# Second attention of a four-stage kernel: maxima reduced two banks at a time, scores in a ring of three banks, exponentials over two banks and one

## The reference, cut to what matters

```python
qkv = x @ attn_qkvw + attn_qkvb            # x: 2 x 256 x 512 in the drawn shapes, here 1 x 1024 x 512
qkv = qkv.reshape(B, S, 3, HEADS, hd)      # 32 heads of 16
scores = jnp.einsum('bhqd,bhkd->bhqk', q, k) * scale
probs = jax.nn.softmax(scores, axis=-1)
ctx = jnp.einsum('bhqk,bhkd->bhqd', probs, v)
return ctx @ attn_ow + attn_ob
```

## Time and profile before

| | us |
|---|---|
| median of 3 runs | 1727.81 (1727.61 to 1731.67) |
| the profiled execution, its own time | 1724.92 |
| its span, first to last instruction | 1722.6 |
| PE busy over the span | 1546.5 (90%) |
| DVE busy | 1038.8 (60%) |
| ACT busy | 809.8 (47%) |
| POOL busy | 227.6 (13%) |

### The profile page before, as it was taken

One profiled execution on the slowest core, in us unless ns is written; L12 is line 12 of the kernel. 1 busy time (PEld: TensorE's weight loads), 2 busy tenths in 40 slices (PEclk: granted clock), 3 DMA queues, 4 the chain that ended last, 5 costly groups with the idle time before them and its releaser, 6 DMA issues. The chain is left out here.

```text
span 1722.6 us, 22663 instructions
## 1 busy us (share of the span) xinstructions
PE 1546.5 (90%) x8286; PEld 1012.5 (59%) x8286; DVE 1038.8 (60%) x1801; ACT 809.8 (47%) x1458; POOL 227.6 (13%) x225
## 2 busy tenths in 40 slices
PE   6958999999999999879799989887799888899987
PEld 4736766776666777568688878666343333333355
DVE  5735666666666666445433335642679777889446
ACT  5325666666666666322112122131047555667834
POOL 2751112111111111000000000000000331131100
PEclk9978999999999999989899999989559988989999
DMA  4242212221111211243121210055712245441001
GB/s 129 97 154 70 69 59 66 68 89 65 65 65 59 84 58 32 80 146 107 64 73 56 73 50 1 2 208 184 109 22 41 62 80 84 84 54 23 18 13 43
DMA packets 71714, 125.23 MB, mean 73 GB/s; under 512 B 13054, under 2 KB 38782, under 8 KB 70318
## 3 DMA queue, kind: packets, MB, share of 16 engines
q1 hardware_dynamic: 71540, 123.67, 25.6%
q0 software_dynamic: 64, 0.11, 0.0%
HBM read 87.23 MB, written 33.85 MB: 70 GB/s over the span
## 5 line engine op out<-in xcount | busy, mean ns | idle before, releaser
L1625 DVE TENSOR_REDUCE ah_minus_half<-ah_ring 128x1 f32<-128x512 f32 x512 | 317.2, 679 | 56.6 <-PE ah_ring L1553 56.6
L1608 ACT ACTIVATE ah_probs<-ah_score 128x1024 f32<-128x1024 f32 x256 | 248.8, 1022 | 179.1 <-PE ah_score L1568 178.5
L958 DVE TENSOR_REDUCE mh_minus_max<-mh_score 128x1 f32<-128x128 f32 (+7 forms) x256 | 193.7, 757 | 195.5 <-PE mh_score L772 195.3
L1553 PE MATMUL ah_ring<-ah_k_stack,ah_q_stack 48*128 48x512 f32 x512 | 216.3, 525 | 54.2 <-DVE ah_minus_half L1625 30.2
L1553 PEld LDWEIGHTS ah_ring<-ah_k_stack,ah_q_stack 48*128 48x128 f32 x512 | 98.2, 211 | 237.9 <-DVE ah_minus_half L1625 211.5
L882 ACT ACTIVATE mh_probs<-mh_score,mh_minus_max 128x128 f32<-128x128 f32 (+7 forms) x256 | 189.6, 741 | 35.9 <-DVE mh_minus_max L958 33.4
L1568 PE MATMUL ah_score<-ah_q_stack,ah_k_stack 49*128 49x512 f32 x512 | 167.1, 466 | 6.5 <-DMA ah_q_stack<-ah_rows 4.9
L768 PE MATMUL mh_score<-shared,h_hi 128*128 128x512 f32 (+3 forms) x384 | 151.6, 395 | 2.2 <-ACT mh_probs L882 2.2
L1583 PE MATMUL ah_mix<-ah_probs,ah_v 128*32 128x512 f32 x1024 | 148.5, 654 | 0.6 <-ACT ah_probs L1608 0.6
L1031 POOL TENSOR_TENSOR h_lo<-mh_pe,h_hi 64x512 fp32r<-64x512 f32 x64 | 81.8, 1279 | 469.5 <-ACT h_hi L868 465.9
L769 PE MATMUL mh_score<-shared,h_hi 128*128 128x512 f32 (+3 forms) x384 | 132.1, 344 | 0.0
(11 more groups left out here) (224 smaller groups left out, 2886.7 us busy)
## 6 DMA issues: line engine op xcount, KB each, us to landing
mh_w<-in_w_pairs SPq DMA_DIRECT2D x16, 896.0 KB, 5.5
x<-in_w_inner SPq DMA_DIRECT2D x14, 768.0 KB, 4.1
pe_scratch<-fr_pe_out SPq DMA_DIRECT2D x4, 2048.0 KB, 6.6
mh_pe<-pe_scratch SPq DMA_DIRECT2D x16, 512.0 KB, 3.9
mh_spread<-inverse_scratch SPq DMA_DIRECT2D x64, 128.0 KB, 2.8
a_scratch<-mh_mixed SPq DMA_DIRECT2D x32, 256.0 KB, 2.3
x<-a_scratch SPq DMA_DIRECT2D x8, 1024.0 KB, 5.8
qk_scratch<-shared SPq DMA_DIRECT2D x32, 256.0 KB, 2.0
```

The costliest lines, as they stand in the source:

```text
L958: nc.vector.reduce_max(minus_max[:, s % 4:s % 4 + 1], score_ps[s % 2][:, base:base + width], AX.X, negate=True).then_inc(max_ready, 1)
L1553: return nc.tensor.matmul(ring[:, m % 3, :], q_stack[a][stack_rows(p, PARTS), c, t * P:(t + 1) * P], k_stack[a][stack_rows(p, PARTS), c, h ...
L1608: nc.scalar.activation(probs[:, 2 * (u % 2) + c, :], score_ps[c][:].rearrange("p e n -> p (e n)"), ACT.Exp, scale=MHA_SCALE).then_inc(prob ...
L1625: nc.vector.reduce_max(minus_half[:, m:m + 1], ring[:, m % 3, :], AX.X, negate=True).then_inc(max_taken, 1)
```

## The change

Three things are edited. The eight banks are dealt out anew: `ah_ring` has four banks as two pairs, `ah_score` has three, `ah_mix` keeps one. A maximum is now taken of two heads at once: two matmuls, one semaphore, one DVE reduction over 2 x 512 columns with two results. The score matmuls are numbered 0 to 511 and go to bank `n % 3`; ACT takes the exponential of banks 0 and 1 together and then of bank 2 alone. `probs` has room for three units instead of two. The lead of the maxima is built up by eight per unit instead of seven, all maxima lie at the starts of the two score stages, and DVE inverts sums four maxima later. Last, `Shares.put` no longer waits until POOL has divided the half-group two before, but until the one four before is divided and the one two before is inverted; `c_in` and `spread_in` get a semaphore per group parity for that.

```diff
@@ Shares.put
         sp.wait_ge(out_taken, NHALF * g + half + 1)
-        wait(sp, self.ready, NHALF * (g - 1) + half + 1)
+        wait(sp, self.ready, NHALF * (g - 2) + half + 1)
+        wait(sp, self.inverse_ready, NHALF * (g - 1) + half + 1)
@@ mha_heads
-        probs = sb("probs", [P, 4, 2 * BANK])
-        ring = ctx.enter_context(nc.psum_tensor("ah_ring", [P, 3, BANK], F32))
-        score_ps = [ctx.enter_context(nc.psum_tensor(f"ah_score{i}", [P, 2, BANK], F32)) for i in range(2)]
+        probs = sb("probs", [P, BANKS, BANK])
+        ring = ctx.enter_context(nc.psum_tensor("ah_ring", [P, 2, 2, BANK], F32))
+        score_ps = ctx.enter_context(nc.psum_tensor("ah_score", [P, 3, BANK], F32))
...
+        exps_before = lambda tiles: 2 * (tiles // 3) + (tiles % 3 > 0)
-            at = lambda unit: min(FIRST + 7 * unit, HALF_MAX + LEAD + PER_UNIT * unit, TOTAL)
+            at = lambda unit: min(FIRST + 8 * unit, HALF_MAX + LEAD + PER_UNIT * unit, TOTAL)
             now, then = at(n), at(n + 1)
-            return (now, min(now + (then - now + 1) // 2, then), min(now + (3 * (then - now) + 2) // 4, then))[stage]
+            middle = min(now + 2 * ((then - now + 2) // 4), then)
+            return (now, middle, middle)[stage]
@@ PE
-            def one_maximum(m):
-                wait(pe, max_taken, m - 2)
-                maximum(m).then_inc(max_ready, 1)
+            def two_maxima(m):
+                wait(pe, max_taken, m // 2 - 1)
+                maximum(m)
+                maximum(m + 1).then_inc(max_ready, 1)
...
-                wait(pe, probs_ready, 2 * (NUNIT * g + u) + c - 1)
                 for p in range(2):
+                    n = 4 * (NUNIT * g + u) + 2 * c + p
                     rows = stack_rows(p, PARTS + 1)
-                    last = nc.tensor.matmul(score_ps[c][:, p, :], k_stack[a][rows, c, j * P:(j + 1) * P],
-                                            q_stack[a][rows, c, half * BANK:(half + 1) * BANK], start=True, stop=True)
-                last.then_inc(scores_ready, 1)
+                    if n >= 3:
+                        pe.wait_ge(probs_ready, exps_before(n - 2))
+                    nc.tensor.matmul(score_ps[:, n % 3, :], k_stack[a][rows, c, j * P:(j + 1) * P],
+                                     q_stack[a][rows, c, half * BANK:(half + 1) * BANK], start=True, stop=True
+                                     ).then_inc(scores_ready, 1)
@@ ACT
+            for n in range(4 * UNITS):
+                if n % 3 == 0:
+                    exp(n, 2)
+                    done = n + 2
+                elif n % 3 == 2:
+                    exp(n, 1)
+                    done = n + 1
@@ DVE
-                nc.vector.reduce_max(minus_half[:, m:m + 1], ring[:, m % 3, :], AX.X, negate=True).then_inc(max_taken, 1)
+                nc.vector.reduce_max(minus_half[:, m:m + 2], ring[:, m // 2 % 2, :, :], AX.X, negate=True).then_inc(max_taken, 1)
...
-                if m >= HALF_MAX * (inverted + 1) + LEAD + 13 * PER_UNIT:
+                if m >= HALF_MAX * (inverted + 1) + LEAD + 14 * PER_UNIT:
```

More of the change, by code:

```diff
@@ L1354, in put @@
             first = rows.start + n * HD
-            sp.dma_start(self.c[first:first + HD, cols], out[2 * HD * n:2 * HD * n + HD, g % 2, cols]).then_inc(self.c_in[half], 16)
+            sp.dma_start(self.c[first:first + HD, cols], out[2 * HD * n:2 * HD * n + HD, g % 2, cols]).then_inc(self.c_in[g % 2][half], 16)
     def free_out(self, act, g, half):
-        wait(act, self.c_in[half], 64 * (g - 1))
+        wait(act, self.c_in[g % 2][half], 64 * (g // 2))
         wait(act, self.sums_in[half], 16 * (g - 1))
@@ L1373, in spread_inverse @@
         heads = self.inverse_rows[g, half].rearrange("(n t) q -> n (t q)", n=4).unsqueeze(1)
-        sp.dma_start(self.spread[rows, cols], heads.to_broadcast([4, HD, BANK])).then_inc(self.spread_in[half], 16)
+        sp.dma_start(self.spread[rows, cols], heads.to_broadcast([4, HD, BANK])).then_inc(self.spread_in[g % 2][half], 16)
     def divide(self, pool, g, half):
@@ L1405, in mha_heads @@
         FIRST = HALF_MAX + 4
+        PAIRS = HALF_MAX // 2
+        BANKS = 12
         STACK_DMAS = 12
@@ L1582, in mix @@
                     rows = slice(32 * head, 32 * head + 32)
-                    last = nc.tensor.matmul(mix_ps[rows, :], v[a][:, j, rows], probs[:, 2 * (u % 2) + c, p * BANK:(p + 1) * BANK],
+                    last = nc.tensor.matmul(mix_ps[rows, :], v[a][:, j, rows], probs[:, 4 * ((NUNIT * g + u) % 3) + 2 * c + p, :],
                                             start=j == 0, stop=j == NT - 1)
@@ L1603, in take_out, with exp @@
                 nc.scalar.copy(out[:, g % 2, half * BANK:(half + 1) * BANK], mix_ps[:]).then_inc(out_taken, 1)
[L1605 to L1608, removed]
-                                     ACT.Exp, scale=MHA_SCALE).then_inc(probs_ready, 1)
-            for g in range(GROUPS):
-                for u in range(NUNIT):
-                    exp(g, u, 0)
-                    exp(g, u, 1)
-                    if u == 0 and g:
-                        take_out(g - 1, 1)
-                    if u == NT:
-                        take_out(g, 0)
+            def exp(n, count):
+                last = n + count - 1
+                act.wait_ge(scores_ready, last + 1)
+                wait(act, mixed, last // 4 - 2)
+                place = n % BANKS
+                nc.scalar.activation(probs[:, place:place + count, :], score_ps[:, n % 3:n % 3 + count, :], ACT.Exp, scale=MHA_SCALE
+                                     ).then_inc(probs_ready, 1)
+            taken = 0
+            for n in range(4 * UNITS):
[5 more added lines that the diff above has]
+                    done = n + 1
+                if taken < NHALF * GROUPS - 1 and done >= 4 * (NT * (taken + 1) + 1):
+                    take_out(*divmod(taken, NHALF))
+                    taken += 1
             take_out(GROUPS - 1, 1)
```

28 lines of the change are left out of this document (14 added, 14 removed).

## The result

The changed kernel takes 1771.36 us (median of 5 runs, 1767.66 to 1774.52) against 1727.81 before: a ratio of 1.0248, 95% interval 1.0227 to 1.027. The forecast was 1748, in a range of 1728 to 1775. The time lies inside the range, but the change is twice the forecast one: +43.6 us against +20.2 in medians. The profiled execution took 1767.66 us, its span is 1765.4, so 42.8 us more than before.

What follows compares the result with a forecast made beforehand. Before the change, a 2.71 us loop per unit, neither PE's nor DVE's own work, was taken as the bound. Steady units +38.8, stalls -28, last units +12, opening -2 gave +21, hence 1748 us, range 1728 to 1775.

Steps and rivals of the forecast that it cites:

- The bound on a unit: Steady units: three score banks make PE wait for exponentials, 3.14 us per unit against 2.71; +38.8 us with joins.
- the last units: Last units, without maxima: the score chain gives 2.89 us each at full clock, against 1.98; +12 us.
- the stalls: Second attention: five waits for sums shrink with longer units and PE's clock does not fall; -28 us, bounds -33.5 and -21.
- the relaxed wait: SP's sums: no longer waiting for POOL is worth nothing, as the copy of `ah_mix` ends later, by 1.0 us.
- the waits for sums: DVE before inverting: sums land late behind SP's queue traffic; 25.5 us in five waits shrink to 12.5 in four.
- case C: Rival for the steady units: pauses keep PE's clock at 1.2 GHz, half of 104 units give +75, 1823 us; chance 0.10.
- the opening: Start of the second attention: net -2 us if the clock rises as late as before, near 1290 us.
- B: Rival for the units: paired maxima pay and scores do not bind, 2.3 us per unit, about 1701 us; chance 0.12.
- D: Rival for the whole kernel: gains and losses meet, with an early clock rise and no stall loss, 1732 us; chance 0.06.

Runs made afterwards that it cites:

- e4: Changed kernel with SP issuing the quarter of weights after the next half-group's sums and rows of maxima: 1755.40 us, ratio 1.0167.
- e2: Changed kernel with the old single-bank maxima in a ring of three, keeping three score banks and exponentials of two and one: 1778.12 us, ratio 1.0297.
- e3: Changed kernel with one exponential per score bank, all else as in the change: 1744.36 us, ratio 1.0116.
- e6: Changed kernel with all four maxima of a unit between its two pairs of scores: 1762.48 us, ratio 1.0193.
- e1: Changed kernel with the old wait for POOL put back in front of the sums: 1767.57 us, ratio 1.0234.
- e7: Kernel before the change, with only the weights issued after the next sums and rows of maxima: 1706.20 us, ratio 0.987.
- e11: Kernel before the change, with weights issued later and the relaxed wait for sums: 1696.58 us, ratio 0.9815.
- e8: Changed kernel with unread matmuls, four per unit, in units 116 to 127: 1757.77 us, ratio 1.0192.
- e5: Changed kernel with the values' product of unit n-2 between the two pairs of scores of unit n: 1785.38 us, ratio 1.0343.
- e10: Changed kernel with maxima between score pairs, one exponential per bank, weights later, and unread matmuls in units 116 to 127: 1689.40 us, ratio 0.9777.

## Why the prediction was wrong

The bound on a unit was right. Two terms of the sum were mis-sized, both by a clock that was taken to stay up: the last units (+25.1 for +12) and the stalls (-19.8 for -28). The reason given for the relaxed wait was wrong as well.

**Right: what bounds a unit.** Each unit type was forecast at 3.28, 3.28 and 2.86 us and measured 3.30, 3.28 and 2.84 (e4, without stalls: 326.7 us for 104 units, 3.14 each). The wait stands where it was put, at the last score of a unit or at both of the second pair. e2 shows that it comes from the three banks and not from the maxima, e3 and e6 that its links can be shortened one by one by the amounts that the rows give. The unit of the kernel before without its waits is (320.1 - 33.5) / 104 = 2.76 with joins, so this term was forecast at +38.8 and is 326.7 - 286.6 = +40.1.

**Right by luck: the relaxed wait is worth nothing here** (e1). The prediction said that the copy of `ah_mix` ends after POOL and hides the wait, and that with slower units POOL's end "falls further behind". The reverse came: in the changed kernel POOL ends after the copy in four half-groups, by 1.0, 2.0, 2.1 and 4.1 us, and the old wait does delay those sums in e1. Nothing is lost because DVE inverts them 16 us later. e7 and e11 show where the relaxed wait is worth 10 us; the prediction had named faster units as the condition, and what brought it about was POOL's later work on the weights.

**Right: the waits for sums come from SP's queue** and shrink with longer units: 5.4, 2.0, 3.0 and 2.3 us remained of 25.5, together 12.7 against 12.5 forecast. e4 takes the weights from in front of the sums, and none remains.

**Wrong: what those waits cost.** The step was "PE pauses too briefly for its clock to fall: -28". In the profile the clock fell after the first (5.4 us) and after the third (3.0 us), and about the third there are four units of 3.9 to 5.0 us. The stalls cost 13.7 us (340.4 less 326.7) where I had 5.5, so the term is -19.8 and not -28, beyond the bound of -21, which had left the clock out. Read from the starts of the products, the two waits without a fall cost 0.8 and 0.5 us, about what I had allowed, and the two with one cost 7.2 and 5.3, of which 6.6 us lie in the five units in which the clock was down.

**Wrong: the last units.** The step was to put 2.89 us on each "at full clock". The first three did take 2.90 on average, but from 1638.8 us the clock was down and units took 4.07, 4.53 and 4.49: +25.1 us instead of +12. The chain itself was right: 2.90 against 2.89 at full clock. e8 settles the cause, since filling the pauses brings the full clock and 11 us back. This was case C in another place. I had priced it for the steady units, where e4 shows no fall in 322 us (e5, with more pauses, had some), and not for the units without maxima, where PE was busy for only 8.7 of 12.8 us before the fall. With 13 of the 22 us it is the larger half of the error.

The section "A second HAM failure mode: psum-queue depth-cycling" of the Trainium skill, page "TensorE: Matmul & The Clock Gate", which the prediction cites, had the right direction for this stretch: small pauses between groups of matmuls, and a clock that fell. But the clock here went down once and stayed at 0.50 for 44.4 us rather than going back and forth.

**Too small: the opening.** -6.5 us against -2, since the clock rose at 1263.4 us (and, after 3.4 us at the low level, for good at 1270.2) and not at 1288.2. It rose among units of eight maxima, so the prediction's reading that only units of four maxima end the slow stretch does not hold. In the runs with the same opening it took from 39.1 to 46.4 us (e4, e8), so this is a draw of some 7 us that nothing here decides. In e8 the clock rose as late as before, at 1287.9 us, and the stretch up to unit 9 took 0.8 us more than before, not 2 less. Another 3.9 us lie outside the attention and were in no term; 2.7 of them stand before its first maximum, whose start lay between 1212.8 and 1218.5 us in the profiles although no edit touches the work before it.

The rivals B and D are out: no unit came near 2.3 us while three banks and exponentials of two were kept. With single-bank exponentials and the other edits of e10, units come to 2.61 us, against 2.71 before.

## What to carry to other kernels

Count a buffer by how long it is held, from the write through the reader to the release, not by how busy its reader is: one bank less for the scores cost 40 us over 104 units while ACT had idle time to spare, and making the reader's pieces smaller or moving independent work between write and release gave back what the chain said. Where a loop leaves PE short pauses, check the stretches with the least work separately: in e4 the clock held through the steady loop, with pauses of 0.9 us, and fell at the end, with pauses of 1.1 us and less work around them. And before a wait is called covered, look at who needs what it delays, and how soon: the same wait cost nothing where DVE came 16 us later, and 10 us where the weights had moved behind the sums.

## What the runs showed of the hardware

- The granted clock fell to 1.2 GHz without any standstill: before the fall in the last units PE was busy for 8.72 of 12.80 us, its longest pause was 1.1 us, and the clock stayed down for 44 us in which PE was busy for 37.3. With unread matmuls in the pauses it stayed at 2.4 GHz (e8).
- After waits of DVE of 2.3 and 1.9 us the clock fell in e7; after 2.0 and 2.3 us it did not in the changed kernel. In e8 it fell after 2.6 and 2.7 us and not after 3.0. The length of the wait alone does not decide it.
- A reduction of 2 x 512 columns from two banks into two results took 1.213 us, no more than 1024 columns into one (1.225).
- The openings of e4 and e8, the same instructions, differed by 7 us (39.1 and 46.4) by when the clock rose: for good at 1268.5 and at 1287.9 us.
